# Alternating the PSUM banks of the attention levels, and putting q updates ahead of the masked copies

## What is computed

```python
def step(S, inp):                       # the scan over 512 tokens, per head
    qt, kt, vt, gt = inp
    S = jnp.exp(gt)[:, None] * S + kt[:, None] * vt[None, :]
    return (S, qt @ S)
o = rmsnorm(scan(q, k, v, g)) * silu(x @ Wg);  attn = o @ Wo
x = x + layernorm(attn_ref(layernorm(x)))
h = gelu(einsum('etd,edf->etf', layernorm(x), w1) + b1)       # 8 experts, two sequences each
x = x + layernorm(einsum('etf,efd->etd', h, w2) + b2)
```

## Time and profile before

| | us |
|---|---|
| median of 3 runs | 1315.18 |
| lowest and highest | 1313.88, 1315.83 |
| the profiled execution's own time | 1313.97 |
| its span in the trace | 1312.2 |
| busy: PE, PEld | 1230.2 (94%), 1073.7 (82%) |
| busy: DVE | 1044.8 (80%) |
| busy: ACT, POOL | 711.3 (54%), 635.0 (48%) |
| mean granted clock of PE | 0.988 of full speed |

### The profile page before, as it was taken

The page is one execution under the profiler, slowest core; times in us unless marked ns, Lnnn a source line. Parts: engine busy times, 40 slices in busy tenths (PEclk is TensorE's granted clock), DMA queues, the critical chain, the costliest instruction groups (busy, mean ns, idle before and its releaser), DMA issues. The chain is left out here.

```text
span 1312.2 us, 23418 instructions
## 1 busy us (share of the span) xinstructions
PE 1230.2 (94%) x8372; PEld 1073.7 (82%) x8372; DVE 1044.8 (80%) x2404; ACT 711.3 (54%) x1443; POOL 635.0 (48%) x893
## 2 busy tenths in 40 slices
PE   5889999999999999999999999999999999999957
PEld 3677889888897888889888788988889888897956
DVE  3769788796978979787787978879697896978863
ACT  5365555656456465644756555565545646465423
POOL 5436353563445544564435635356354554456431
PEclk9989999999999999999999999999999999999988
DMA  3110010100101001010011001010010100100000
GB/s 97 38 33 17 17 49 1 54 17 17 49 21 49 1 17 49 21 49 1 17 49 53 16 17 49 1 54 16 17 49 21 48 2 17 49 21 33 1 17 17
DMA packets 31778, 38.27 MB, mean 29 GB/s; under 512 B 2448, under 2 KB 29104, under 8 KB 31664
## 3 DMA queue, kind: packets, MB, share of 16 engines
q1 hardware_dynamic: 31136, 36.25, 8.3%
q10 hardware_dynamic: 528, 0.52, 0.1%
HBM read 28.38 MB, written 8.39 MB: 28 GB/s over the span
## 5 line engine op out<-in xcount | busy, mean ns | idle before, releaser
L1047 POOL TENSOR_TENSOR k_decayed<-k_decayed,block_totals 128x256 f32<-128x256 f32 x192 | 168.2, 876 | 277.1 <-PE ps_level L298 276.6
L298 PEld LDWEIGHTS ps_level<-q_blockdiag,k_decayed 128*128 128x128 f32 x1792 | 227.1, 191 | 51.5 <-DVE q_blockdiag L585 41.1
L298 PE MATMUL ps_level<-q_blockdiag,k_decayed 128*128 128x128 f32 x1792 | 241.1, 278 | 26.4 <-DVE q_blockdiag L585 25.1
L575 DVE COPY_PREDICATED attn_T<-level_masks,ps_level 128x512 f32<-128x512 uint32 x160 | 152.7, 954 | 16.0 <-PE ps_level L298 16.0
L585 DVE TENSOR_TENSOR q_blockdiag<-q_blockdiag,block_totals 128x512 f32<-128x512 f32 x192 | 141.3, 736 | 28.1 <-PE ps_level L298 28.1
L1053 POOL TENSOR_TENSOR rstd<-rstd,minus_half 128x1 f32<-128x1 f32 x192 | 111.7, 584 | 106.6 <-DVE rstd L636 106.6
L255 PE MATMUL ps_big<-w_ff_hi,h_hi 128*128 128x256 f32 x512 | 150.1, 293 | 3.0 <-DVE h_lo L590 3.0
L257 PE MATMUL ps_big<-w_ff_hi,h_lo 128*128 128x256 f32 x512 | 144.8, 283 | 0.0
L256 PE MATMUL ps_big<-w_ff_lo,h_hi 128*128 128x256 f32 x512 | 144.7, 283 | 0.0
L837 ACT ACTIVATE gelu_out<-ps_big,ff_b_cols 128x512 f32<-128x512 f32 x128 | 88.0, 688 | 79.8 <-PE ps_big L257 43.2
L623 DVE SCALAR_TENSOR_TENSOR o<-o,o_rstd,out_gate 128x128 f32<-128x128 f32 x256 | 93.3, 426 | 45.0 <-POOL o_rstd L1068 45.0
(11 more groups left out here) (113 smaller groups left out, 3155.1 us busy)
## 6 DMA issues: line engine op xcount, KB each, us to landing
w_raw<-L_ffn_w SPq DMA_DIRECT2D x16, 1024.0 KB, 5.6
out<-y SPq DMA_DIRECT2D x16, 512.0 KB, 2.9
x_in<-L_attn_x SPq DMA_DIRECT2D x15, 512.0 KB, 3.9
ff_b_rows<-L_ffn_b SPq DMA_DIRECT2D x8, 128.0 KB, 2.6
x_in<-L_attn_x ACTq DMA_DIRECT2D x1, 512.0 KB, 4.0
w_raw<-L_attn_Wv SPq DMA_DIRECT2D x1, 512.0 KB, 6.0
w_raw<-L_attn_Wg SPq DMA_DIRECT2D x1, 512.0 KB, 7.1
y<-L_attn_Wo SPq DMA_DIRECT2D x1, 512.0 KB, 8.1
```

The lines of the kernel that those rows point to most:

```text
L298: last = nc.tensor.matmul(PL[tl][:, c * CH:(c + 1) * CH], kk[:, tl, c * CH:(c + 1) * CH], q[:, :, :, 1, :], start=True, stop=True)
L575: nc.vector.copy_predicated(dst, m.to_broadcast([P, 2 * NCH, HC // h, h]), src)\
L1047: nc.gpsimd.tensor_tensor(k, k, t.to_broadcast([P, n, h]), ALU.mult)\
```

## The change

There are four edits. (1) Odd levels are written to the banks `ps_out` and `ps_state` and even levels to `ps_level`, so `level(i, tl)` waits for the masked copy of level i-2 instead of i-1. `diag_rows` and `diag_columns`, which used `ps_out`, now use `ps_transpose0` and `ps_transpose1`; `diag_rows` goes ahead of the first level, and `diag_columns` from step 3 to step 1, ahead of the transposes `x3t`, the second of which now waits for DVE's copy of the diagonal. (2) DVE does the q update of a step first, and the masked copy of the step before behind it. (3) ACT's block copies of levels 5 and 6 wait until all ten masked copies are done. (4) POOL's four `weight_lo` of odd runs are in steps 5 to 8 instead of 1 to 4.

```diff
+        LVB = [PL, [PO, PS]]
 # tensor engine, level(i, tl)
-                            if C:
-                                pe.wait_ge(sem["dv_o"], at("dv_o", p, NCH * H))
...
-                        if i - 1 < MASKED:
-                            pe.wait_ge(sem["dv_cp"], at("dv_cp", s, 2 * (i - 1) + tl + 1))
-                        else:
-                            pe.wait_ge(sem["ac_cp"], at("ac_cp", s, 2 * tl + 2))
+                        if i >= 2:
+                            pe.wait_ge(sem["dv_cp"], at("dv_cp", s, 2 * (i - 2) + tl + 1))
+                        elif C and tl == 0:
+                            pe.wait_ge(sem["dv_o"], at("dv_o", p, NCH * H))
+                        elif C:
+                            pe.wait_ge(sem["dv_st"], at("dv_st", p, states(NCH - 1)))
...
-                        last = nc.tensor.matmul(PL[tl][:, c * CH:(c + 1) * CH],
+                        last = nc.tensor.matmul(LVB[i % 2][tl][:, c * CH:(c + 1) * CH],
 # tensor engine, diagonal
+                    if C:
+                        pe.wait_ge(sem["dv_oglo"], at("dv_oglo", p, NCH - 1))
+                    else:
+                        pe.wait_ge(c_ready, 3)
+                    pe.wait_ge(sem["dv_q"], at("dv_q", s, 2 * KT - 1))
...
-                            last = nc.tensor.matmul(PO[32 * c:32 * (c + 1), 0:CH], ind[:, tl, :],
+                            last = nc.tensor.matmul(PT[0][32 * c:32 * (c + 1), 0:CH], ind[:, tl, :],
...
-                    nc.tensor.transpose(PO[:, CH:2 * CH], o[:, 0, 0:CH], ident[:, :]).then_inc(sem["pe_diag"], 1)
+                    if C:
+                        pe.wait_ge(sem["dv_oglo"], at("dv_oglo", p, NCH))
+                    nc.tensor.transpose(PT[1][:, 0:CH], o[:, 0, 0:CH], ident[:, :]).then_inc(sem["pe_diag"], 1)
 # x3t(kt)
+                    if B and kt:
+                        pe.wait_ge(sem["dv_dg"], at("dv_dg", s, 1))
 # st(c)
+                    pe.wait_ge(sem["ac_cp"], at("ac_cp", s, 6))
 # tensor engine, steps
                     if B:
+                        if step == 0:
+                            diag_rows()
                         level(step // 2, step % 2)
                         if step == 1:
-                            diag_rows()
-                        if step == 3:
                             diag_columns()
 # vector engine, steps
-                    if B and step == 4:
-                        dve.wait_ge(sem["pe_diag"], at("pe_diag", s, 1))
...
                     if B:
-                        if step // 2 < MASKED:
-                            copy_pairs(step // 2, step % 2)
                         q_update(step // 2, step % 2)
+                        if step == 1:
+                            dve.wait_ge(sem["pe_diag"], at("pe_diag", s, 1))
...
                     if C:
                         if step == 1:
                             for kt in range(KT):
                                 lo_part(xT_lo[:, kt, :], xT_hi[:, kt, :], PT[kt][:, :], "ac_x3hi", p, kt + 1, "dv_x3lo")
+                    if B and 1 <= step <= 2 * MASKED:
+                        copy_pairs((step - 1) // 2, (step - 1) % 2)
+                    if C:
                         if 4 <= step < 4 + FT:
 # scalar engine, copy_blocks
+                    act.wait_ge(sem["dv_cp"], at("dv_cp", s, 2 * MASKED))
 # GpSimd, steps
-                    if C and j == 1 and 1 <= step < 5:
-                        weight_lo(1, step - 1, e)
+                    if C and j == 1 and 5 <= step < 9:
+                        weight_lo(1, step - 5, e)
```

More of the change, by code:

```diff
@@ L571, in copy_pairs @@
                     dve.wait_ge(sem["pe_lv"], at("pe_lv", s, 2 * i + tl + 1))
+                    if i + tl:
+                        dve.wait_ge(sem["dv_cp"], at("dv_cp", s, 2 * i + tl))
                     dst = Am[:, tl, :, :].rearrange("p a (n t h) -> p a n t h", t=2, h=h)[:, :, :, 1, :]
-                    src = PL[tl][:, :].rearrange("p (a n h) -> p a n h", a=2 * NCH, h=h)
+                    src = LVB[i % 2][tl][:, :].rearrange("p (a n h) -> p a n h", a=2 * NCH, h=h)
                     m = masks[:, i, :].bitcast(U32).rearrange("p (a n h) -> p a n h", a=1, h=h)
@@ L717, in run @@
                 for step in range(2 * NL):
-                    if B and step == 4:
-                        dve.wait_ge(sem["pe_diag"], at("pe_diag", s, 1))
-                        nc.vector.tensor_copy(dg[:, :].rearrange("p (c h) -> p c h", h=H),
-                                              PO[:, CH:2 * CH].rearrange("p (c r) -> p c r", r=32)[:, :, 0:H])\
-                            .then_inc(sem["dv_dg"], 1)
                     if B:
-                        if step // 2 < MASKED:
-                            copy_pairs(step // 2, step % 2)
                         q_update(step // 2, step % 2)
+                        if step == 1:
+                            dve.wait_ge(sem["pe_diag"], at("pe_diag", s, 1))
+                            nc.vector.tensor_copy(dg[:, :].rearrange("p (c h) -> p c h", h=H),
+                                                  PT[1][:, 0:CH].rearrange("p (c r) -> p c r", r=32)[:, :, 0:H])\
+                                .then_inc(sem["dv_dg"], 1)
                     if C:
@@ L856, in copy_blocks @@
                         copy(Am[r, tl, :, 2 * h * b + h:2 * h * (b + 1)],
-                             PL[tl][r, :].rearrange("p (a n h) -> p a n h", a=2 * NCH, h=h)[:, :, b, :], "ac_cp")
+                             LVB[i % 2][tl][r, :].rearrange("p (a n h) -> p a n h", a=2 * NCH, h=h)[:, :, b, :], "ac_cp")
                 def squares(c):
@@ L897, in run @@
                     act.wait_ge(sem["pe_drow"], at("pe_drow", s, 1))
-                    copy(o[:, 0, 0:CH], PO[:, 0:CH], "ac_dg")
+                    copy(o[:, 0, 0:CH], PT[0][:, 0:CH], "ac_dg")
                 if C:
```

## The result

The changed kernel takes 1327.52 us (median of 4 runs, 1326.9 to 1329.27) against 1315.27 for the kernel before. The ratio is 1.0097, with a 95% interval of 1.0079 to 1.0114: it is slower by 12.25 us, where 1317 (1303 to 1324) was forecast. Its profiled execution took 1327.55, with a span of 1325.8; that of before had taken 1313.97, 1.3 under its median. In what follows two disturbed runs of free_early (1374 and 3061 us) and one of the kernel before (3061) are left out.

A forecast was written before the change was run, and what follows sets the result against it. PE, busy 94%, was taken to bound the kernel, but DVE in odd stages; terms -0.7 + 2.8 + 0.7 = +2.8 us on the profiled 1313.97 gave 1316.8, as median 1318.0. Predicted 1317, range 1303 to 1324.

The forecast's parts named there:

- the walk: Step-by-step count of DVE's queue through a stage, with work, idle time and POOL meetings up to the eighth low part.
- Odd stage +0.4: Eighth low part in odd stages ends at 30.0 against 29.64: +0.4 in seven stages, +2.8 us.
- even stage -0.1: Eighth tile in even stages, between +0.17 and -0.33: taken as -0.1 in seven stages, -0.7 us.
- s = 15 +0.7: Last odd stage, without statistics: its chain from last masked copy through block copies and gelu to low part costs +0.7.
- s = 0 0: Stage without feed-forward work: diag_rows delay DVE by 0.6, its short waits for PE go; 0, bounds -0.6 and +0.6.
- 1.09 + 23.2 + 1.2 idle + 4.5 meetings = 30.0: Odd stage's DVE queue: start, work, idle time and nine meetings with POOL, to the end of the eighth low part.
- 1.09 + 23.2 + 1.0 + 2.8 = 28.1: Even stage's DVE queue: start, work, idle time and meetings with POOL, to the end of the eighth low part.
- -0.33: Even stage, step 10: if the order of k update and low part goes the other way, the stage ends at 684.7.
- 5.85 and 5.65: Forecast starts of the first feed-forward product after the stage's start, odd and even: 1.8 and 1.2 earlier than before.
- hides in the statistics: ACT's block copy, put behind the last masked copy by edit 3, was to cost nothing except in s = 15.
- Rival 2: Late weight instructions land in the busiest steps: 1.0 more in each odd stage, 8 us, 1325; chance 0.22.
- the old places cost 2.0 too: Argument against slower late weights: POOL's weight instructions in steps 1 to 4 already cost 2.0.

The follow-up runs named there:

- free_early: Changed kernel with the statistics behind the eighth low part, gelu before ACT's block copies, and POOL's weight instructions back in steps 1 to 4; 1304.6 us.
- stats_late: Changed kernel with DVE's four statistics instructions moved from step 10 to behind the eighth low part in step 11; 1325.49 us.
- gelu_first: Changed kernel with ACT's gelu and high part ahead of its block copies of levels 5 and 6 in a step; 1325.42 us.
- weights_early: Changed kernel with edit 4 alone undone: POOL's four weight instructions back in steps 1 to 4; 1318.81 us.
- before_late: Kernel before with edit 4 alone: POOL's four weight instructions of an odd stage in steps 5 to 8; 1314.96 us.
- copy_first: Changed kernel with each masked copy again ahead of the q update of its step, banks, diagonal and weights as changed; 1349.63 us.
- copy_first_diag: Changed kernel with each masked copy ahead of the q update of its step, and DVE's diagonal copy ahead of both in step 1; 1320.83 us.
- before_free: Kernel before with the statistics behind the eighth low part and gelu before ACT's block copies; 1312.82 us.

## Why the prediction was wrong, by its own steps

**Right.** The mechanism and its place: PE loses the waits for q updates, DVE's queue has nothing to give and takes the time back, and it shows as a wait for the low part (forecast about 20 us, measured 16.7; 1.5 at each eighth tile forecast, 1.41 measured in odd stages and 0.84 in even ones). In the odd stage PE's levels of steps 7 to 10 fall back by 0.17, 0.46, 0.45 and 0.44 (757.11, 759.85, 762.58 and 765.30 against a step of 2.28), 1.5 in all, as the walk had it; its 0.8 at `diag_columns` was 0.20. The second transpose waits 0.77 for the diagonal copy in the even stage (0.7 forecast); four low parts of an even stage, steps 6 to 9, take 1.13 to 1.15 (1.1 forecast), each with a k update that starts just ahead. Both orders occur: h_lo takes 1.15 behind a k update, and w_ff_lo 1.73 behind a q update. The Trainium skill's rule (SBUF — State Buffer, "Who interferes with whom": of two such instructions the first to start keeps the shared ports for its length) agrees with these rows. In step 10 of the even stage it can't be read off the starts: the k update's row starts 0.03 ahead (688.87 and 688.90), and yet the low part takes 0.67 and the k update 1.18.

**Wrong: the sizes of the stage terms, all on one side.** Odd stage +0.4 forecast, +0.8 measured; even stage -0.1, and +0.2; s = 15 +0.7, and +1.4; s = 0 0, and +0.85. Where the walk slipped can be read from its own sum, with the meetings counted one by one in DVE's timeline (each by what an instruction takes over 0.68).
- *Odd.* Forecast 1.09 + 23.2 + 1.2 idle + 4.5 meetings = 30.0. Measured: start 0.99 (743.16), idle 0.38 + 0.21 + 0.47 + 0.28 = 1.34, meetings 0.35 (744.86), 0.13, 0.84 (754.47) and seven of 0.44 to 0.47, together 4.5. The eighth low part ends at 30.44, which leaves 23.6 for the work itself.
- *Even.* Forecast 1.09 + 23.2 + 1.0 + 2.8 = 28.1. Measured: 0.99, idle 0.38 + 0.21 + 0.71 = 1.30, meetings 0.35, 0.1 and four of 0.46, with a few hundredths 2.4, end 28.24: again 23.55 for the work.
- So the meetings of the odd stage were right and those of the even one 0.4 too high (in step 10 the low part got in first, the case to which I had given -0.33). Wrong was the work, 0.35 to 0.4 too low in both. I had summed start-to-start spacings (0.60 for an instruction of 0.69), but in front of a wait an instruction counts with its full length, and this queue has four waits in the odd stage and three in the even one; the rest is a q update of 0.64 here and there. Against a forecast change of 0.4, an error of 0.35 in a sum of 23 is everything. The rows of the kernel before could have shown it, but only in the even stage. Its odd stage has no wait in this queue, and its meetings, counted one by one, are the 5.3 that the sum left over; the even one has five waits, and of the 3.4 left over only 3.0 are meetings and idle time.
- The idle time of the even stage was 0.3 more. The k update of level 0 is itself longer (0.88 each in the pair of the earlier trace rows) than the later ones (0.64 at 679.75); I had read these 0.88 as the length of any k update without a meeting, and 1.02 as one with it. The second q update, behind such a pair, takes 1.04, and with it the diagonal copy, the second transpose and the tokens' low parts are 0.3 late. The first product starts at 6.16 where I had 5.85 and 5.65; of the even stage's 0.5 this covers 0.3, and 0.2 stay open.

**Wrong: edit 3's cost "hides in the statistics".** It hides only in the sense that both chains are equally long. stats_late and gelu_first gain 2.0 and 2.1 us alone and 16.2 together. A cover of exactly the same length as what it hides is no slack, and I had costed the last copy's move from the queue of DVE only, except at s = 15. There the cover is missing, and gelu_first shows it: tile 29.19 against 30.37, 1.18 in one stage.

**The nearest rival was near by luck.** Rival 2 (1325, chance 0.22) wanted PE's levels to fall back 1.0 more in each odd stage than the walk had. They fell back by the walk's own 1.5, and the odd meetings were the walk's 4.5, so the late weights stood in the sum at their size. What neither the sum nor a rival had is that in this order the old places are cheaper, by 1.14 an odd stage (weights_early). I had set the two places equal ("the old places cost 2.0 too"), which is true for the old order (before_late: 0) and false for the new one.

**Not in the sum at all:** 0.09 at the first product of each of 14 stages (1.3 us), and the stage of s = 0, where I took the middle of -0.6 to +0.6 and +0.85 came. Each is small; with the stage terms they all go up. The sum itself gave 1318.0, and 1317 was taken. The upper end, 1324, was 1 below rival 2 (1317 + 8) and had no room for the terms left out.

Open: why s = 0 takes longer (0.85, or 0.6 by the last section); no experiment was made for it. The 1.2 behind the last stage go with the time at half clock there, and both orders of instructions occur with the short time and with the long one (last section); whether the change makes the long one more frequent, one trace of each kernel can't tell.

## What to carry to other kernels

When a change removes waits on one engine, price it at the next place where that engine must wait for all of the others' work, here the eighth tile, and look there for every chain that ends within a few tenths of the last: only freeing all of them lets the gain through (2.0, 2.1, together 16.2 us). A moved instruction has no price of its own; moving the same four weight instructions cost 0 or 8.7 us, by the order of the queue that they meet. And a short instruction on which the bound engine waits (the 0.16 us copy of the diagonal) goes ahead of long ones: in one order that was worth 28.8 us, in another 3.5.

## What the runs showed of the hardware

- A wait of PE of 2.87 us in copy_first, at the same place of each even stage, was followed by half clock: both level groups behind it take 1.92 and 1.85 us, against 1.08 and 1.07 in the changed kernel, where PE's wait at that place is 0.77. The window shows it (length, busy PE, PEld, DVE, ACT, POOL, then the granted clock, 0.50, that is 1.2 GHz, and the DMA share):

```profile
843.30:846.72 3.42, 3.42 (x19) 3.42 (x17) 2.13 (x4) 0.60 (x1) 0.74 (x1) 0.50 0.00 0
```

  All seven even stages have it, and in copy_first_diag, with a wait of 1.16, none. The two groups take 1.92 + 1.85 - 1.08 - 1.07 = 1.6 us more. From start to start the even stages are 2.28 longer than in copy_first_diag and the odd ones 0.99, so by an estimate 1.3 of the 1.6 remain in each, 9 us of the 28.8 that the place of the diagonal's copy makes.
- The length of one wait doesn't decide it. In the odd stages of copy_first the same wait is 2.46, and one of eight (s = 1) fell to half clock. In the kernel before, waits of 1.17 or 1.18 and 0.56 stand at the start of each odd stage, and one of eight (s = 7) fell:

```profile
584.96 2.07 PE L298 MATMUL ps_level<-q_blockdiag,k_decayed 128*128 128x128 f32 x8 [0.56 <-DVE q_blockdiag L585]
```

  Its first product starts at 8.42 instead of 7.67, but its tile is at 29.92 instead of 29.70, and the next stage starts 0.16 late: where DVE is the engine without a gap, a slow PE costs little.
- Behind the stage of s = 0 the profiled execution of the kernel before has a half-clock stretch of 6.83 us, that of the changed kernel one of 10.24 (the same window, before first):

```profile
66.17:73.00 6.83, 4.75 (x18) 3.96 (x19) 3.36 (x5) 2.07 (x4) 0.90 (x1) 0.50 0.00 1
```

```profile
66.25:76.49 10.24, 7.30 (x24) 5.93 (x25) 4.71 (x7) 2.75 (x5) 1.77 (x2) 0.50 0.00 0
```

  All ten experiments show the longer one, before_free and before_late, with the old start, among them. So these 1.3 us of the span look like the luck of one execution, which also stands 1.3 under its median; and 13.6 - 1.3 = 12.3 us of span agree with the 12.25 us between the medians. before_late runs s = 0 as the kernel before does, and takes 68.04 from the start of its stage to that of s = 1, against 66.52 in the kernel before and 68.66 in the changed one: by that the stretch is worth 1.5, and 0.6 are left for the change.
- From the eighth tile of s = 15 to the end of the span, the time goes with the time at half clock behind the last level stage (without the half clock in which the span ends): 78.2 to 78.5 us with 10.24 of it, 79.4 to 80.1 with 13.65, 80.7 and 80.8 with 17.07, 82.1 with 20.48. Both orders stand in the first group (before_late 78.17, stats_late 78.52) and in the third (before_free 80.73, the changed kernel 80.83). The kernel before has 13.65 and 79.60.
